# Products of zeros on TensorE while it waits in the norms of two self attentions and in the output block of the second cross attention

## What is computed

```python
x = x + _L0_xattn_ref(_layernorm(x), ctx_2048, ...)   # cross attention, 32 heads, normed queries and keys
x = x + _L0_attn_ref(_layernorm(x), ...)              # self attention, 16 heads, low-rank additions
x = x + _L0_ffn_ref(_layernorm(x), ...)               # mixture of 16 experts, best 2, and 2 shared
x = x + _L1_xattn_ref(_layernorm(x), ctx_2048, ...)   # cross attention, 16 heads, queries and output rounded to 255 steps
x = x + _L1_attn_ref(_layernorm(x), ...)              # self attention, 32 heads, 8 of keys, masked
x = x + _L1_ffn_ref(_layernorm(x), ...)               # mixture of 32 experts, best 8
```

## Time and profile before

| | |
|---|---|
| median of 3 runs | 1483.12 us (1482.01 to 1488.65) |
| the profiled execution | 1493.27 us |
| its span, first to last instruction | 1491.5 us |
| mean granted clock of TensorE in it | 0.957 |
| PE busy | 1390.7 us, 93% of the span |
| DVE, ACT, POOL busy | 68%, 52%, 5% |

### The profile page before, as it was taken

One profiled execution on the slowest core, in us unless ns is written; L12 is line 12 of the kernel. 1 busy time (PEld: TensorE's weight loads), 2 busy tenths in 40 slices (PEclk: granted clock), 3 DMA queues, 4 the chain that ended last, 5 costly groups with the idle time before them and its releaser, 6 DMA issues. The chain is left out here.

```text
span 1491.5 us, 31870 instructions
## 1 busy us (share of the span) xinstructions
PE 1390.7 (93%) x11742; PEld 1074.0 (72%) x11742; DVE 1006.9 (68%) x1659; ACT 778.2 (52%) x1134; POOL 78.4 (5%) x71
## 2 busy tenths in 40 slices
PE   6999999999969889999989999969999588999998
PEld 4677776777735489999977877846666355899997
DVE  7666676666636467666547777768999644676664
ACT  3777777777732455454432322327888113455542
POOL 0000000000011300000011111110000100000000
PEclk9999999999989989999999999978999669899999
DMA  5443544333232087656125332237775111676662
GB/s 162 86 92 91 124 104 86 85 84 84 50 113 105 1 266 267 211 181 213 36 58 183 107 130 100 84 89 167 170 170 128 55 43 56 204 232 215 212 210 74
DMA packets 133599, 191.20 MB, mean 128 GB/s; under 512 B 74987, under 2 KB 96717, under 8 KB 130317
## 3 DMA queue, kind: packets, MB, share of 16 engines
q1 hardware_dynamic: 133533, 190.30, 44.3%
HBM read 154.12 MB, written 17.48 MB: 115 GB/s over the span
## 5 line engine op out<-in xcount | busy, mean ns | idle before, releaser
L187 PE MATMUL psum<-m_x_hi,m_gu_hi 128*128 128x256 f32 x780 | 223.1, 286 | 2.1 <-DVE m_h L2404 1.8
L188 PE MATMUL psum<-m_x_hi,m_gu_lo 128*128 128x256 f32 x780 | 222.6, 285 | 0.0
L189 PE MATMUL psum<-m_x_lo,m_gu_hi 128*128 128x256 f32 x780 | 222.5, 285 | 0.0
L1544 DVE TENSOR_REDUCE x_peaks<-psum 128x2048 f32 (+1 forms) x64 | 146.3, 2291 | 50.4 <-PE psum L1422 50.4
L187 PEld LDWEIGHTS psum<-m_x_hi,m_gu_hi 128*128 128x128 f32 x780 | 151.1, 194 | 5.7 <-DVE m_h L2404 2.2
L188 PEld LDWEIGHTS psum<-m_x_hi,m_gu_lo 128*128 128x128 f32 x780 | 151.0, 194 | 1.5
L187 PE MATMUL psum<-x_w_hi,x_ctx_hi 128*128 128x256 f32 x512 | 151.9, 297 | 0.0
L189 PEld LDWEIGHTS psum<-m_x_lo,m_gu_hi 128*128 128x128 f32 x780 | 151.0, 194 | 0.0
L504 ACT ACTIVATE x_probs<-psum 128x1024 f32<-128x1024 f32 x128 | 124.1, 1022 | 45.9 <-PE psum L394 45.8
L504 ACT ACTIVATE x_w_raw<-psum 128x1024 f32<-128x1024 f32 x128 | 124.2, 1025 | 41.3 <-PE psum L394 37.3
L188 PE MATMUL psum<-x_w_hi,x_ctx_lo 128*128 128x256 f32 x512 | 144.9, 283 | 0.0
(11 more groups left out here) (319 smaller groups left out, 2826.3 us busy)
## 6 DMA issues: line engine op xcount, KB each, us to landing
m_gu_raw<-in_m_gu SPq DMA_DIRECT2D x41, 768.0 KB, 4.3
e_w<-x_keys_dram SPq DMA_DIRECT2D x45, 512.0 KB, 6.8
m_gu_raw<-in_m_gu SPq DMA_DIRECT2D x18, 1024.0 KB, 4.9
x_ctx_raw<-in_ctxT SPq DMA_DIRECT2D x64, 256.0 KB, 2.8
m_dn_raw<-in_m_down SPq DMA_DIRECT2D x16, 768.0 KB, 4.3
m_dn_raw<-in_m_down SPq DMA_DIRECT2D x18, 512.0 KB, 5.2
x_keys_dram<-x_keys_hi SPq DMA_DIRECT2D x16, 512.0 KB, 3.2
x_keys_dram<-e_wqp SPq DMA_DIRECT2D x16, 512.0 KB, 2.7
```

The lines of the kernel that those rows point to most:

```text
L187: pe.matmul(out, a[0], b[0], start=start, stop=False, skip_group_check=True)
L188: pe.matmul(out, a[1], b[0], start=False, stop=False, skip_group_check=True)
L189: return pe.matmul(out, a[0], b[1], start=False, stop=stop, skip_group_check=True)
L1544: dve.tensor_reduce(peaks[:, t, 4 * m:4 * m + 4, bass.ds(k, 1)].rearrange("p h k -> p (h k)"), g.psum[:, at:at + BANKS, :], AX, ALU.max).t ...
```

## The change

A helper `keep_busy` issues `count` products of `g.zeros` by itself, 128 by 128 weights and 512 columns in bf16, into a bank of PSUM that nobody reads. It is called at four places: 8 products ahead of PE's first wait in the norm of the first self attention, 4 in that of the second, both into bank 7; and in the output block of the second cross attention 6 ahead of the wait for the grid of tile 0 and 4 ahead of the wait for that of tile 1, into bank 3. No wait, no semaphore and no other engine's work changes.

```diff
+def keep_busy(pe, g, bank, count):
+
+    for _ in range(count):
+        pe.matmul(bank, g.zeros[:, 0:P], g.zeros[:, :], start=True, stop=True, skip_group_check=True)
...
-        stage_layernorm(nc, g, "ln_a0_", prefetch)
+        stage_layernorm(nc, g, "ln_a0_", prefetch, True, lambda pe: keep_busy(pe, g, g.bank[7], 8))
...
-        stage_layernorm(nc, g, "ln_a1_", prefetch)
+        stage_layernorm(nc, g, "ln_a1_", prefetch, True, lambda pe: keep_busy(pe, g, g.bank[7], 4))
...
                     for t in range(NT):
+                        keep_busy(pe, g, g.bank[3], (6, 4)[t])
                         pe.wait_ge(step_done, GRID_STEPS[-1] * (t + 1))
                         pe.wait_ge(wp_row_taken, 1)
```

## The result

| | before | changed |
|---|---|---|
| median | 1487.33 us (20 runs, 1481.8 to 1490.84) | 1491.32 us (20 runs, 1485.39 to 1497.42) |
| ratio | | 1.0031, 95% interval 1.0021 to 1.0041 |
| profiled execution | 1493.27 us | 1493.35 us |
| its span, mean granted clock | 1491.5 us, 0.957 | 1491.5 us, 0.961 |

The account below looks back on a forecast made before the run. The prediction took TensorE's clock, halved in and after idle time around both norms, as the cost. Terms -1.6 (first norm), -0.7 (output block) and 0 (second norm) gave -2.3 us, 1483.1 to 1480.8 us, range 1476.5 to 1487.

Parts of the forecast that it names:

- Behind the keys PE works at full clock and sets the end of the stage, so all of this reaches the end: First self attention: the whole -1.6 us won ahead of the keys was claimed to reach the end.
- a term of -1.6: First self attention's norm: 8 zeros bring the clock back sooner, so the keys start earlier; -1.6 us, bounds -1.8 and +0.9.
- a term of -0.7: Output block: the clock returns before the second zeros, removing DVE's waits of 0.26 and 0.47 us; -0.7 us.
- The slower bound of +1.9: Output block: at half clock all the way, the zeros delay the second transposes and what follows by +1.9 us.
- a rule on transposes: Output block: transposes do not count as busy like matmuls, giving +1.9 instead of -0.7 and a sum of +0.3 us.
- The second norm: Second self attention's norm: the clock falls again before the keys, so the term is 0, bounds -2.2 and +0.1 us.
- rival (a): The clock, back in the output block, holds into the second norm and keys: -4.5 us in all, 1478.4; chance 0.20.
- Rival (b): Zeros cost more than they bring, delaying transposes in output block and first norm: +2.9 us, 1486.0; chance 0.15.

Follow-up runs that it names:

- after: The changed kernel with all 22 products of zeros, against the kernel before, in its first trace: median 1491.32 us, ratio 1.0031; profiled execution 1493.35 us.
- a0_out: Zeros in the first norm and the output block, those of the second norm left out, against the kernel before: 1484.17 us, 0.9982.
- a0_out2: The kernel with zeros in the first norm and output block only, run once more for its trace: 1482.72 us in one run.
- all_a0filled: The changed kernel plus 8 zeros in the wait for the first self attention's key weight and 6 behind its values: 1488.31 us, 1.0002 to the kernel before.
- after2: The changed kernel, unaltered, measured again with a second trace: 1491.38 us, 1.0033 to the kernel before.
- after3: The changed kernel, unaltered, run once more for a third trace: 1488.84 us in one run.
- out_a1_filled: Zeros in output block and second norm, plus 8 in the second self attention's wait for placed keys, against the kernel before: 1482.52 us, 0.9969.
- all_filled: The changed kernel plus fillers at the first self attention's two waits and the second's wait for placed keys: 1483.29 us, 0.9973 to the kernel before.
- out_a1: Zeros in the output block and the second norm, those of the first norm left out, against the kernel before: 1485.96 us, 0.9989.
- a0_only: Only the 8 zeros in the first self attention's norm, against the kernel before: 1486.25 us, 0.9993.
- a0_filled: First norm's 8 zeros, plus 8 in the wait for the keys' weight and 6 behind the values, against the kernel before: 1491.65 us, 1.0026.
- a1_only: Only the 4 zeros in the second self attention's norm, against the kernel before: 1486.09 us, 0.999.

## Why the prediction was wrong

**Where the sum failed.** It failed at the step "Behind the keys PE works at full clock and sets the end of the stage, so all of this reaches the end". The sum counted what an earlier end of the `a_down` products brings until the weight's landing, and named that landing as the bound, but took the wait that opens in front of it as free. It was not: PE waits 1.3 to 2.5 us there, and in five of seven traces the clock fell again behind it or at the scores. Up to the keys the term was right: in after they start 1.5 us sooner behind the Block's start than in the trace of before, for a term of -1.6. At the end of the stage it is, in the three traces of the changed kernel, 92.2 - 90.6 = +1.6 on average. Where the clock did not fall again (a0_out, a0_out2) the stage is 0.9 us shorter than the mean, so what is won does reach the end there. all_a0filled, which only fills these waits, takes 3 to 4 us off the changed kernel, though its trace does not show that it is by this fall.

**The base was on the long side, too.** The keys of before start 14.2 us behind the Block in its first trace, but 13.4 to 13.7 in seven of ten traces with this stage unaltered (14.2 in three). So mostly 0.6 to 0.9 us could be won up to the landing, not 1.8. The 1493.27 us of that execution should have warned of it, and 3 runs were few for a level: 17 more moved the median by 4.2 us, more than the change was forecast to bring.

**The output block: right.** From its first operation to the next norm it took 19.5 us in all seven traces without its zeros at full width, the delayed ones aside, and 18.6 to 18.8 in the eleven with them: -0.75 to -0.95 for a term of -0.7. The clock came back between the two groups of zeros and DVE's two waits went, as written. The slower bound of +1.9, which the prediction also tied to a rule on transposes, was never seen; the row that shows the four zeros in 1.03 us decides against that bound. The Trainium skill, "TensorE: Matmul & The Clock Gate", Part 4 (PE-mode transpose), says that transposes do not count as busy in the way matmuls do; no run here had transposes alone, so the rule itself is neither shown nor refuted.

**The second norm: the forecast right in name, wrong in what it leaves.** In the four traces with all three groups and nothing ahead of the tops (after, after2, after3, all_a0filled) the keys ran at full clock, as rival (a) had it, though the clock had fallen and come back in between, and the tops started 15.4 to 16.3 us behind the Block's start instead of 17.0 to 17.2. The prediction let this "pass to the end, since the loading back of the keys ends last". Beside the output block it gave, with the tops at half clock, less than nothing on average: kernels with the output block's zeros took 76.3 to 76.8 us for the stage in four traces without the second norm's zeros, and 76.0 to 79.4 in five with them and nothing ahead of the tops. It is the same mistake as in the first norm, at the second wait for a DMA. The filler brings 3.4 us (out_a1_filled) and 5.0 us (all_filled). This is a loss beside the output block's zeros alone, not beside the kernel before, whose two traces have 80.9 and 79.4 us for the stage.

**The rivals.** Rival (b) has the right sign, and a size near it, +2.9 for +4.0, but by luck, for its mechanism is another: the zeros in front of the second transposes cost nothing, and what costs is the waits that the time saved opens.

**What stays open.** The traces locate losses, but they do not add up to the 4 us: the spans of the three traces of the changed kernel average 1489.0 us, those of two of before 1488.8. By their averages the first self attention costs 1.6 us, the output block brings 0.9, and the last mixture took 230.4 to 230.5 us in all three traces of the changed kernel but 226.8 and 230.9 in two of before. With single executions differing by 5 us in stages that no change touches, a trace or three cannot settle 1 us. Why adding the first norm's zeros costs 5.4 us beside both other groups (out_a1 to after2) and nothing measurable on its own is told in part by the wait behind the norm, from which a0_out is spared; a0_only, whose trace shows the full loss of 3.8 us in this stage and whose median is still 1 us below before, does not fit. Its runs reach from 1480.6 to 1493.1, so it may be spared in some; that was not measured. Nor does a0_filled fit, with 5.4 us more for fillers that took 3 to 4 off the changed kernel.

**Better kernels than both.** out_a1_filled, 1482.5 us, is 0.31% faster than before (0.17% to 0.45%); the changed kernel is 0.31% slower. The output block's zeros alone (0.9965 and 0.9981), a0_out (0.9982) and all_filled (0.9973) have intervals that overlap with its own, so the fillers are not shown to beat the simplest of these.

## What to carry to other kernels

A product of zeros in front of a wait can move the idle time of TensorE: what it gains in clock ends at the next wait for a transfer or another engine, and the clock can fall there instead. Before counting such a gain, look for the next wait behind it; fill that as well or leave the place alone, and measure the whole kernel, since the same filler helped one kernel here and not another. The output block's zeros alone did as well here as any group with fillers. And check that the profiled execution is an ordinary one before taking terms from it, above all where it is slower than every timed run.

## What the runs showed of the hardware

- The clock fell where TensorE had only short pauses: behind one wait of 1.97 us, with the border of Blocks of 0.93 us ahead of it (after2, at 444.0), and 0.9 to 1.8 us into the tops behind a wait of 1.57 to 2.56 us (before, after, out_a1, a1_only). The tops themselves, most of whose products use 16 of 128 rows, did not bring it down in six traces with at most 0.89 us of idle time ahead of them (12.7 us from first to last round, against 17.4 to 18.4).
- Once down, it stayed at half for 23.9 us in the tops of after while PE was busy 21.78 of 23.7 us, and for 3.4 or 6.8 us behind the first products of the keys in the first self attention.
- Products of zeros by zeros do hold the clock up: eight of them in the wait ahead of the tops (1.67 us for the seven recorded) took the tops from 17.8 to 12.7 us (out_a1, out_a1_filled), and from 17.6 to 12.7 in all_filled against all_a0filled.
- Executions of one kernel differ by up to 12 us (1485.39 to 1497.42), and in their traces by falls of the clock in stages that are the same code.
